# Two sums counted apart and a new order of stages in a two-layer graph attention kernel

## The reference

```python
scores = jnp.where(mask, -1e+18, jnp.einsum('bod,bid->boi', q, k) / denom)
attn = jnp.where(mask, 0.0, jax.nn.softmax(scores, axis=2))
x = node_fts + jnp.einsum('boi,bie->boe', attn, node_fts) @ Wc   # then layer norm
```

```python
logits = jnp.einsum('bhqd,bhkd->bhqk', q, k) / np.sqrt(DK)
logits = logits + jnp.log(jnp.clip(adj, ADJ_MIN, None))[:, None, :, :]
out = jnp.einsum('bhqk,bhkd->bhqd', jax.nn.softmax(logits, axis=-1), v)
```

## Time and profile before

| | |
|---|---|
| Three executions, us | 1279.22, 1281.15, 1282.41 (median 1281.15) |
| The profiled execution | 1281.39 us, span 1279.6 us, mean granted clock 0.97 |
| One mixed phase | about 74.5 us |
| Busy share | TensorE 92%, VectorE 72%, GpSimd 57%, ScalarE 41% |

### The profile page before, as it was taken

The page is one execution under the profiler, slowest core; times in us unless marked ns, Lnnn a source line. Parts: engine busy times, 40 slices in busy tenths (PEclk is TensorE's granted clock), DMA queues, the critical chain, the costliest instruction groups (busy, mean ns, idle before and its releaser), DMA issues.

```text
span 1279.6 us, 21166 instructions
## 1 busy us (share of the span) xinstructions
PE 1177.2 (92%) x6474; PEld 693.0 (54%) x6474; DVE 927.5 (72%) x1735; ACT 525.0 (41%) x1020; POOL 726.4 (57%) x352
## 2 busy tenths in 40 slices
PE   6889999999999999999999999999999999999883
PEld 5555465655646565564646556464655646465431
DVE  4465877868687786867778686877858687795875
ACT  2233444444344444434444443444444344444431
POOL 0016477483747748385674738567474856747472
PEclk8889999999999999999999999999999999999977
DMA  3041331404132140413214041321404223150310
GB/s 124 1 124 42 99 83 39 127 17 134 47 98 74 41 131 17 131 49 94 70 47 134 17 127 54 91 73 43 138 17 120 61 86 78 40 141 17 74 42 17
DMA packets 69652, 94.67 MB, mean 74 GB/s; under 512 B 14081, under 2 KB 32769, under 8 KB 69634
## 3 DMA queue, kind: packets, MB, share of 16 engines
q1 hardware_dynamic: 69634, 94.44, 25.8%
HBM read 35.40 MB, written 8.39 MB: 34 GB/s over the span
## 4 chain that ended last, share of the span: by engine, by line
issue 34%; POOL 33%; PE 19%; DVE 10%; ACT 2%; POOLq 1%; DMA 1%; DVEq 0%; SPq 0%; ACTq 0%
POOL PR L1145 22%; PE misc L598 5%; PE values L742 3%; PE scores L719 3%; POOL z L1159 3%; DVE mx L1006 3%; POOL res L1128 3%; POOL rstd L1136 2%; POOL z L1161 2%; PE misc L698 2%; DVE CLIP L979 1%; DVE z L1087 1%; DVE xn L1045 1%; PE misc L676 1%; DVE sums_v L1058 1%
## 5 line engine op out<-in xcount | busy, mean ns | idle before, releaser
L1145 POOL TENSOR_TENSOR PR<-PR,CLIP 128x1024 f32<-128x1024 f32 x217 | 536.6, 2491 | 463.8 <-ACT PR L853 463.8
L853 ACT ACTIVATE PR<-scores 128x512 f32<-128x512 f32 x512 | 279.0, 601 | 334.3 <-PE scores L719 327.1
L1006 DVE TENSOR_REDUCE mx<-misc 128x1 f32<-128x512 f32 x512 | 320.8, 677 | 105.2 <-PE misc L698 104.8
L719 PE MATMUL scores<-QS,KS 97*128 97x512 f32 x512 | 201.1, 465 | 8.9 <-issue 3.4
L742 PE MATMUL values<-PR,V 128*32 128x512 f32 x1024 | 133.5, 605 | 22.5 <-POOL PR L1145 11.0
L698 PE MATMUL misc<-K1H,Q1H 32*128 32x512 f32 x512 | 129.4, 502 | 16.6 <-DVE Q1L L970 8.7
L719 PEld LDWEIGHTS scores<-QS,KS 97*128 97x128 f32 x512 | 89.4, 195 | 98.8 <-ACT PR L853 52.8
L742 PE MATMUL denominators<-PR,ones 128*32 128x512 f32 x1024 | 133.4, 604 | 0.6 <-DVE z L1071 0.3
L698 PEld LDWEIGHTS misc<-K1H,Q1H 32*128 32x128 f32 x512 | 55.2, 184 | 129.3 <-DVE mx L1006 49.0
L676 PE MATMUL misc<-U,P 128*128 128x257 f32 x512 | 120.2, 383 | 0.0
L1053 DVE RECIPROCAL sums_w<-sums_w 128x128 f32<-128x128 f32 x128 | 114.1, 925 | 7.7 <-ACT sums_w L863 4.5
(11 more groups left out here) (159 smaller groups left out, 1904.4 us busy)
## 6 DMA issues: line engine op xcount, KB each, us to landing
ADJ<-adj_t SPq DMA_DIRECT2D x16, 1024.0 KB, 5.6
QS<-Q1H SPq DMA_DIRECT2D x256, 64.0 KB, 2.0
KS<-K1H SPq DMA_DIRECT2D x256, 64.0 KB, 2.0
P<-x_t SPq DMA_DIRECT2D x16, 512.0 KB, 3.6
X<-x SPq DMA_DIRECT2D x16, 512.0 KB, 3.5
QS<-Q1L SPq DMA_DIRECT2D x128, 64.0 KB, 2.0
KS<-K1L SPq DMA_DIRECT2D x128, 64.0 KB, 2.0
out<-z SPq DMA_DIRECT2D x16, 512.0 KB, 2.9
```

Source lines behind the costliest of these rows:

```text
L719: pe.matmul(ST[n][:], KS[:, h, P * k:P * (k + 1)], QS[:, h, :], start=True, stop=True).then_inc(scores_filled, 1)
L853: act.activation(PR[quad % WEIGHT_BUFFERS][:, h, :], ST[n][:], ACT.Exp, scale=SCALE1).then_inc(exp_done, 1)
L1006: dve.tensor_reduce(mx1[:, g, h, t:t + 1], misc_bank(ph, "max1", g, n)[:], AX.X, ALU.max, negate=True).then_inc(misc_drained["dve"], 1)
L1145: pool.tensor_tensor(w, w, clipped, ALU.mult).then_inc(masked_pool, 1)
```

## The change

Each of the two sums has its own two semaphores: one for the finished product (`values_summed`, `denominators_summed`), one for the copy (`values_out`, `denominators_out`). The stage `sums_out` is split into `sums_v` and `sums_w`, which may stand apart and in either order. Each copy now states what it overwrites: sums_v waits for low_output, sums_w for normalise; in a phase with a tail they do so for group 0 too. An exponential into a PR buffer waits for both sums of the quad that used it. Reciprocals wait for sums_w alone, normalise for sums_v as well. With this freedom the list of the mixed phase is in a new order; `FIRST` is not touched, and `LAST` only has the two copies by their names.

```diff
@@ -71,28 +71,28 @@
 ]
 SCHEDULE = [
-    ("reciprocal", 1, 0), ("max1", 1, 0), ("split", 0), ("split", 1), ("reciprocal", 1, 1),
-    ("reciprocal", 1, 2), ("max1", 1, 1), ("q0", 0), ("q0", 1), ("bias",), ("scores1", 0, 0), ("u", 0),
-    ("scores1", 0, 1), ("u", 1), ("scores1", 1, 0), ("u", 2), ("reciprocal", 1, 3), ("max0", 0),
-    ("max0", 1), ("scores1", 1, 1), ("normalise", 1), ("max0", 2), ("u", 3), ("skip_back",), ("floor",),
-    ("low_output", 1), ("max1", 1, 2), ("max1", 1, 3), ("max1", 1, 4), ("high_output", 1), ("max0", 3),
-    ("project",), ("scores1", 2, 0), ("skip_back",), ("max1", 1, 5), ("shift0",), ("stats1",),
-    ("max1", 1, 6), ("values1", 0), ("values1", 1), ("denominators1", 0), ("norm1",), ("scores0", 0),
-    ("scores1", 2, 1), ("scores0", 1), ("scores0", 2), ("max1", 1, 7), ("max1", 1, 8), ("output",),
-    ("max1", 1, 9), ("scores0", 3), ("scores1", 3, 0), ("max1", 1, 10), ("max1", 1, 11), ("max1", 1, 12),
-    ("max1", 1, 13), ("denominators1", 2), ("denominators1", 1), ("values1", 2), ("max1", 1, 14),
-    ("max1", 1, 15), ("residual",), ("scores1", 3, 1), ("context0", 0), ("mrow1", 1), ("context0", 1),
-    ("context0", 2), ("scores1", 4, 0), ("mask", 4, 0), ("values1", 3), ("scores1", 4, 1), ("skip_back",),
-    ("context0", 3), ("skip_front",), ("scores1", 5, 0), ("denominators1", 3), ("sums_out", 0), ("stats0",),
-    ("values1", 4), ("scores1", 5, 1), ("denominators1", 4), ("norm0",), ("mask", 5, 0),
-    ("reciprocal", 0, 0), ("reciprocal", 0, 1), ("scores1", 6, 0), ("transpose", 0), ("scores1", 6, 1),
-    ("transpose", 1), ("reciprocal", 0, 2), ("reciprocal", 0, 3), ("values1", 5), ("scores1", 7, 0),
-    ("q1", 0), ("k1", 0), ("normalise", 0), ("q1", 1), ("max1", 0, 0), ("max1", 0, 1), ("max1", 0, 2),
-    ("denominators1", 5), ("max1", 0, 3), ("scores1", 7, 1), ("values1", 6), ("max1", 0, 4), ("max1", 0, 5),
-    ("max1", 0, 6), ("max1", 0, 7), ("denominators1", 6), ("clip",), ("k1", 1), ("denominators1", 7),
-    ("max1", 0, 8), ("max1", 0, 9), ("max1", 0, 10), ("high_output", 0), ("values1", 7), ("low_output", 0),
-    ("max1", 0, 11), ("max1", 0, 12), ("sums_out", 1), ("v", 0), ("max1", 0, 13), ("max1", 0, 14),
-    ("max1", 0, 15), ("v", 1), ("mrow1", 0),
+    ("reciprocal", 1, 0), ("skip_back",), ("split", 0), ("split", 1), ("max1", 1, 0), ("reciprocal", 1, 1),
+    ("max1", 1, 1), ("q0", 0), ("q0", 1), ("scores1", 0, 0), ("bias",), ("u", 0), ("reciprocal", 1, 2),
+    ("scores1", 0, 1), ("u", 1), ("scores1", 1, 0), ("reciprocal", 1, 3), ("u", 2), ("max0", 0),
+    ("normalise", 1), ("scores1", 1, 1), ("max0", 1), ("u", 3), ("high_output", 1), ("max0", 2),
+    ("scores1", 2, 0), ("low_output", 1), ("max0", 3), ("max1", 1, 2), ("max1", 1, 3), ("scores1", 2, 1),
+    ("floor",), ("project",), ("skip_back",), ("max1", 1, 4), ("max1", 1, 5), ("shift0",), ("max1", 1, 6),
+    ("stats1",), ("max1", 1, 7), ("values1", 0), ("values1", 1), ("max1", 1, 8), ("max1", 1, 9),
+    ("denominators1", 0), ("scores0", 0), ("scores0", 1), ("skip_back",), ("output",), ("scores0", 2),
+    ("scores1", 3, 0), ("scores0", 3), ("norm1",), ("max1", 1, 10), ("residual",), ("max1", 1, 11),
+    ("max1", 1, 12), ("denominators1", 1), ("denominators1", 2), ("max1", 1, 13), ("max1", 1, 14),
+    ("max1", 1, 15), ("context0", 0), ("scores1", 3, 1), ("mrow1", 1), ("context0", 1), ("context0", 2),
+    ("scores1", 4, 0), ("values1", 2), ("scores1", 4, 1), ("mask", 4, 0), ("context0", 3),
+    ("scores1", 5, 0), ("denominators1", 3), ("sums_w", 0), ("stats0",), ("norm0",), ("reciprocal", 0, 0),
+    ("values1", 3), ("denominators1", 4), ("reciprocal", 0, 1), ("scores1", 5, 1), ("sums_v", 0),
+    ("transpose", 0), ("mask", 5, 0), ("scores1", 6, 0), ("values1", 4), ("transpose", 1),
+    ("scores1", 6, 1), ("skip_front",), ("values1", 5), ("reciprocal", 0, 2), ("reciprocal", 0, 3),
+    ("q1", 0), ("k1", 0), ("normalise", 0), ("scores1", 7, 0), ("denominators1", 5), ("max1", 0, 0),
+    ("max1", 0, 1), ("max1", 0, 2), ("scores1", 7, 1), ("q1", 1), ("high_output", 0), ("max1", 0, 3),
+    ("max1", 0, 4), ("max1", 0, 5), ("denominators1", 6), ("clip",), ("values1", 6), ("max1", 0, 6),
+    ("max1", 0, 7), ("k1", 1), ("max1", 0, 8), ("denominators1", 7), ("max1", 0, 9), ("max1", 0, 10),
+    ("values1", 7), ("max1", 0, 11), ("max1", 0, 12), ("max1", 0, 13), ("v", 0), ("max1", 0, 14),
+    ("sums_w", 1), ("max1", 0, 15), ("low_output", 0), ("v", 1), ("mrow1", 0), ("sums_v", 1),
 ]
 LAST = [
...
-    ("mask", 4, 1), ("mask", 5, 0), ("denominators1", 3), ("sums_out", 0), ("scores1", 6, 0),
+    ("mask", 4, 1), ("mask", 5, 0), ("denominators1", 3), ("sums_v", 0), ("sums_w", 0), ("scores1", 6, 0),
...
-    ("sums_out", 1), ("low_output", 0),
+    ("sums_v", 1), ("sums_w", 1), ("low_output", 0),
 ]
 ORDERS = {"first": FIRST, "steady": SCHEDULE, "last": LAST, "end": SCHEDULE}
@@ -141,7 +141,7 @@
     "skip_back": None, "skip_front": None,
 }
-BACK = ("residual", "mask", "scores1", "values1", "denominators1", "sums_out",
+BACK = ("residual", "mask", "scores1", "values1", "denominators1", "sums_v", "sums_w",
         "reciprocal", "normalise", "high_output", "low_output", "skip_back")
 TAIL = ("project", "stats1", "norm1", "output")
 SPLIT = ("q0", "transpose", "q1", "k1")
@@ -381,8 +381,10 @@
         masked_pool = sem("masked_pool")
         masked_dve = sem("masked_dve")
-        quad_summed = sem("quad_summed")
-        sums_out = sem("sums_out")
+        values_summed = sem("values_summed")
+        denominators_summed = sem("denominators_summed")
+        values_out = sem("values_out")
+        denominators_out = sem("denominators_out")
         normalised = sem("normalised")
         output_high = sem("output_high")
         output_low = sem("output_low")
@@ -735,7 +737,7 @@
                         pe.wait_ge(misc_drained["act"], misc.count_before(ph, "v", 1))
                 if quad > 0 and k == 0:
-                    pe.wait_ge(sums_out, (ph.i * GROUPS + g) * 2 - (1 if bank is PV else 0))
+                    pe.wait_ge(values_out if bank is PV else denominators_out, ph.i * GROUPS + g)
                 for h in range(PER_GROUP):
                     c = DK * (PER_GROUP * g + h)
                     w = V[:, k, c:c + DK] if bank is PV else ones[:, 0:DK]
@@ -748,16 +750,10 @@
                 return order.index(("values1", quad)) < order.index(("denominators1", quad))
             def values1(ph, quad):
-                first = values_first(ph, quad)
-                mm = sums1(ph, quad, PV, first)
-                if not first:
-                    mm.then_inc(quad_summed, 1)
+                sums1(ph, quad, PV, values_first(ph, quad)).then_inc(values_summed, 1)
             def denominators1(ph, quad):
-                first = not values_first(ph, quad)
-                mm = sums1(ph, quad, DEN, first)
-                if not first:
-                    mm.then_inc(quad_summed, 1)
+                sums1(ph, quad, DEN, not values_first(ph, quad)).then_inc(denominators_summed, 1)
             def project_out(ph):
                 terms = products(Wo1, (OTH, OTL))
@@ -846,21 +842,25 @@
                 if quad >= WEIGHT_BUFFERS and pair == 0:
-                    act.wait_ge(quad_summed, ph.i * QUADS + quad - WEIGHT_BUFFERS + 1)
+                    act.wait_ge(values_summed, ph.i * QUADS + quad - WEIGHT_BUFFERS + 1)
+                    act.wait_ge(denominators_summed, ph.i * QUADS + quad - WEIGHT_BUFFERS + 1)
                 for n in range(2):
                     h = 2 * pair + n
                     act.wait_ge(scores_filled, ph.i * TILES + PER_GROUP * quad + h + 1)
                     act.activation(PR[quad % WEIGHT_BUFFERS][:, h, :], ST[n][:], ACT.Exp,
                                    scale=SCALE1).then_inc(exp_done, 1)
-            def copy_sums(ph, g):
-                act.wait_ge(quad_summed, ph.i * QUADS + (g + 1) * T)
-                if g > 0:
-
-
+            def copy_values(ph, g):
+                act.wait_ge(values_summed, ph.i * QUADS + (g + 1) * T)
+                if g > 0 or ph.tail:
                     act.wait_ge(output_low, ph.i * GROUPS + g)
-                act.copy(sums_v[:], PV[:]).then_inc(sums_out, 1)
-                act.copy(sums_w[:], DEN[:]).then_inc(sums_out, 1)
+                act.copy(sums_v[:], PV[:]).then_inc(values_out, 1)
+
+            def copy_denominators(ph, g):
+                act.wait_ge(denominators_summed, ph.i * QUADS + (g + 1) * T)
+                if g > 0 or ph.tail:
+                    act.wait_ge(normalised, ph.i * GROUPS + g)
+                act.copy(sums_w[:], DEN[:]).then_inc(denominators_out, 1)
             def high_output(ph, g):
@@ -880,7 +880,7 @@
                 "q1": lambda ph, c: hi(ph, "q1", c, Q1H, BQ1),
                 "k1": lambda ph, c: hi(ph, "k1", c, K1H, BK1),
                 "v": lambda ph, n: rows_out(ph, "v", n, V),
-                "scores1": exp1, "sums_out": copy_sums,
```

(4 more changed lines are left out.)

## The result

The changed kernel takes 1231.26 us (median; 1230.28 to 1234.74), the kernel before 1280.85 beside it: a ratio of 0.9617, 95% interval 0.959 to 0.9643. The forecast was 1235.0, range 1218 to 1269. The profiled execution took 1230.28 us (span 1228.5).

A forecast was written before the change was run, and what follows sets the result against it. TensorE, busy 92% of the span, was taken as the bound, with only waits moving. Named places gave 2.65 us, small steps 0.55: 3.2 a phase, 44.8 over fourteen plus 1.6 for the first, so 1281.4 - 46.4 = 1235.0; range 1218 to 1269.

The forecast's parts named there:

- seam: Between two phases: q0 starts 0.5 us later, but XTL comes sooner and its first half ends earlier; gain 0.65 us.
- small steps: Unplaced steps such as the row DMA's wait and fewer product switches: between nothing and 1.0 us, taken as 0.55.
- scores0, 1.5: Scores0 stretch: scores0 0 to 2 stand together and max1 groups take banks drained earlier; gain 1.5 us a phase.
- Copies, 0.7: At values1.4: its 0.71 us wait for sums_v goes, as denominators1.4 comes first; gain 0.7 us.
- Group 0, 0.8 - 0.45: Group 0 to the end: smaller max1 groups wait less, gain 0.8 us; a 13th max1 group costs 0.45.
- Later, -0.55: Norm0 causes 0.4 us of waiting, values1.5 waits about 0.8 for VectorE's mask instead of 0.64; together -0.55 us.
- Clock: Rival: phases at the lower clock, thought five, become none (-7 us, 1228) or all fifteen (+14, 1249); upper case 0.07.
- The freed places fill again: Rival: max1 groups and v wait for VectorE's drains; half the gain lost, 1258 us (0.08), or all, 1281 (0.05).
- clip: Slower rival: clip waits for GpSimd's last mask, forecast done 0.3 us before; 5 us late gives 1302 us; chance 0.07.
- Mask 5.0 too late: Rival: VectorE reaches mask 5.0 after GpSimd's mask 6.0 began; 2.35 us a phase, 1268 us; chance 0.11.

The follow-up runs named there:

- second half: Old order up to context0.2 without values1.2, the change's new order from scores1.4.0 on, copies apart: 1263.3 us, 0.9852 of the kernel before.
- both halves: Two kernels, each with the change's new order on one side of context0.2 and the old order on the other: first half 1254.0 us, second 1263.3 us.
- mask 5.0 late: The change with mask 5.0 moved behind the low part of transpose.1 in VectorE's queue: 1288.6 us, 1.0052 of the kernel before.
- three moves: The change with mask 5.0 before the reciprocals, sums_v.1 and low_output.0 early, and group 1's first reciprocal behind split: 1251.1 us.
- the old order with the new counters: The changed code with the old order of stages, sums_v and sums_w side by side where sums_out stood: 1281.9 us, 0.9994 of the kernel before.
- normalise first: The three moves kernel with normalise of group 1 put in front of max0's first reduction: 1218.4 us, 0.9504 of the kernel before.

## Why the prediction was right

**The frame** held: TensorE's period sets the time and the change only moves waits. Forecast 71.3 us, measured 71.38; sum 46.4, measured 45.3 without the clock's 5.6. The median came out 3.7 us and the profiled execution 4.7 us under 1235: my gain was 1.1 too high, and the clock's 5.6, which I had left as they were, came on top. The per-place terms were less good than their sum. By stretches (starts on TensorE, medians of 13 phases, values1.2 and scores1.7.0 counted where they stood before) the change gained:

| stretch | forecast | measured |
|---|---|---|
| seam | 0.65 | 0.50 |
| q0's second half to scores1.4.0 | 1.5 | 1.13 |
| scores1.4.0 to q1.0 (copies, transpose, mask 5.0) | 0.7 - 0.55 = 0.15 | 0.76 |
| q1.0 to mrow1.0 (group 0) | 0.8 - 0.45 = 0.35 | 0.76 |
| small steps, without a place | 0.55 | |

The first two were too high by 0.5 together and the next two too low by 1.0; the 0.55 without a place happened to make up the difference. That 3.2 came so close to 3.13 is in part luck. Term by term:

- *Seam, 0.65:* 0.5. From mrow1 to q0's second half it takes 3.53 us (654.58 to 658.11) instead of 4.03. q0 starts behind ScalarE's copy as forecast, but its first half takes 1.79 us, not 1.55: its second matmul needs the second part of XTH, cast one after the other by ScalarE. I had only counted XTL.
- *scores0, 1.5:* mis-sized. I took 1.68 us for each scores0, the step of one that followed a scores1. Side by side one takes 1.86 (606.54 to 608.40), and part of what I had read as a wait in the 2.13 of before was this step. The second and third with the idle time behind them took 1.68 + 2.13 + 0.25 us before and take 1.86 + 1.85 now: 0.35 gained, not 0.70. The 1.5 less these 0.35 is near the 1.13 that the stretch gave.
- *Copies, 0.7:* the wait is gone as forecast; but in the old order its going was worth nothing, as values1.5 waited for GpSimd's mask behind it.
- *Group 0, 0.8 - 0.45:* too low. I had left out that denominators1.5's place, with a wait of 0.56 for Q1L behind it, was gaining too: 1.63 to 1.16 us, as q1.1 now stands behind the group of three max1. This is the 8.7 us line that vanished from the list of waits, and the largest single reason why the second half didn't break even. TensorE's timeline before, then after:

```profile
592.03 1.06 PE L742 MATMUL denominators<-PR,ones 128*32 128x512 f32 x8
593.66 0.50 PE L698 MATMUL misc<-K1H,Q1H 32*128 32x512 f32 x1 [0.56 <-DVE Q1L L970]
...
638.88 1.06 PE L744 MATMUL denominators<-PR,ones 128*32 128x512 f32 x8
640.04 0.69 PE L700 MATMUL misc<-K1H,Q1H 32*128 32x512 f32 x3
```

- *Later, -0.55:* too much. values1.5 waits 0.95 (I had 0.8; 0.64 before). transpose.0 is 0.2 us longer, where I had 0.4, but transpose.1 is 0.2 shorter, so the two together cost nothing. That leaves some 0.3. The six scores1 of this stretch take 0.26 less between them (4.34 to 4.08), a small step that I had not placed.
- *Clock:* I wrote that five phases of before had the lower clock. There are four, so the gain of losing all of them is 5.6 us, not the rival's 7; no other term rested on it.

**The rivals.** *The freed places fill again* did not come: both halves kept their gain. *clip* kept 0.8 us of distance, more than the 0.3 I gave it. *Mask 5.0 too late* had the right mechanism and a wrong price. I had 2.35 us a phase and 1268; the kernel with mask 5.0 late lost 3.83 and took 1288.6, since the clock falls behind its wait. So the case to which I gave 0.11 was one of a slower kernel, outside the range. The range was drawn to hold this case and would not have held it. It did not come because the margin was 0.68 us, not 0.2 to 0.5.

## What to carry to other kernels

Where one engine is near its end and only waits move, take them as differences between starts, not from idle columns; and take a step's length from a row with the same neighbour as it will have. Where VectorE's products and GpSimd's masks meet, what counts is who comes first: 0.2 us behind a mask's start cost 2 us, and one stage put 0.55 us sooner gave it back. A long wait on TensorE can cost more than itself (that of 3.25 us here, 1.5 us more), so price it with the lower clock behind it. And a wait that goes gains nothing where the next one hangs on a date that doesn't move: in the old order values1.5 took back all that values1.4 gained.

## What the runs showed that I had not expected

One wait of 3.25 us on TensorE in each phase brought the lower clock in 14 of 14 whole phases. Waits of at most 1.2 us in the kernel with three moves and of 0.8 us in the kernel before had it in 4 phases of their profiles, and the old order with the new counters had it in none. Two operations that don't run side by side show it in both directions: VectorE's multiplication took 2.77 us in the three moves, where the same operation with GpSimd idle took 0.68 (at 639.91 in the changed kernel), and GpSimd's second mask in the changed kernel ended 5.72 us after the first one's start, against 4.70 for a pair that nothing held (above, mask 5.0 late). The VectorE operation that waited at the first mask's end went ahead of GpSimd's second. The pair, in GpSimd's timeline:

```profile
630.93 5.72 POOL L1146 TENSOR_TENSOR PR<-PR,CLIP 128x1024 f32<-128x1024 f32 x2 [1.85 <-ACT PR L850]
```

The Trainium skill (SBUF — State Buffer, section SBUF: two separate sides) calls it a lock on a shared port pair for a whole instruction; the times of arrival in the three moves and in normalise first, on either side of a mask's start, agree with that.
